# Layer two's norm and modulation inside its linear attention; layer one's output, norm and gate logits as one stage by tiles

## What is computed

```python
x = L0_attn_X
h = _layernorm(x, axis=-1) * (1 + ca) + sa
x = x + ga * _L0_attn_ref(h, ...)          # differential softmax attention, 16 heads of two maps
h = _layernorm(x, axis=-1) * (1 + cb) + sb # (A) layer one's second norm
x = x + gb * _L0_ffn_ref(h, ...)           # its experts: softmax(h @ wg), top 1024 tokens of each expert
...                                        # layer two: sa, ca, ga, sb, cb, gb from L1_c
h = _layernorm(x, axis=-1) * (1 + ca) + sa
x = x + ga * _L1_attn_ref(h, ...)          # linear attention
h = _layernorm(x, axis=-1) * (1 + cb) + sb # (B) layer two's second norm
x = x + gb * _L1_ffn_ref(h, ...)           # top-1 experts: softmax(h @ wg)

# end of _L0_attn_ref
O = jnp.einsum('bhqk,bhkd->bhqd', softmax(A1) - lam * softmax(A2), V)
rms = jnp.sqrt(jnp.mean(O * O, -1, keepdims=True) + EPS)
O = O / rms * rms_scale * (1.0 - LAMBDA_INIT)
return O.transpose(0, 2, 1, 3).reshape(B, N, H * 2 * dh) @ W_o.T
```

## Time and profile before

| what | us |
|---|---|
| median of 3 runs (3873.89 to 3878.0) | 3877.72 |
| the profiled execution | 3881.68 |
| its span, first to last instruction | 3879.9 |
| attention0, first DMA to the end of its last PE work | 229 to 2327 |
| out0, first DMA to the first of gates0 | 195.79 |
| gates0, first DMA to the first DVE instruction of route0 | 69.44 |
| linear1, first DMA to the first of gates1 | 230.4 |
| gates1, first DMA to the first instruction of route1 | 64.38 |

### The profile page before, as it was taken

One profiled execution on the slowest core, in us unless ns is written; L12 is line 12 of the kernel. 1 busy time (PEld: TensorE's weight loads), 2 busy tenths in 40 slices (PEclk: granted clock), 3 DMA queues, 4 the chain that ended last, 5 costly groups with the idle time before them and its releaser, 6 DMA issues. The chain is left out here.

```text
span 3879.9 us, 84027 instructions
## 1 busy us (share of the span) xinstructions
PE 3364.8 (87%) x27565; PEld 1836.3 (47%) x27567; DVE 2309.8 (60%) x5396; ACT 1639.4 (42%) x3358; POOL 1690.8 (44%) x1101
## 2 busy tenths in 40 slices
PE   7958999999999999999999995753799958985993
PEld 3413444444444444444444435642455536764662
DVE  4567777777777777777777715767311155665103
ACT  2514656565656565656666661110122235321110
POOL 1413656565656565656566673300344440211103
PEclk9968999999999999999999997855799979995996
DMA  5531111111111111111111104110433320002323
GB/s 180 196 108 25 48 39 42 40 39 43 37 43 36 45 34 46 33 48 31 50 32 47 31 10 144 47 45 0 126 82 78 59 58 5 1 6 95 100 92 97
DMA packets 229266, 224.78 MB, mean 58 GB/s; under 512 B 88722, under 2 KB 198547, under 8 KB 222739
## 3 DMA queue, kind: packets, MB, share of 16 engines
q1 hardware_dynamic: 213522, 194.34, 17.0%
q0 software_dynamic: 15360, 25.44, 3.4%
HBM read 138.58 MB, written 80.35 MB: 56 GB/s over the span
## 5 line engine op out<-in xcount | busy, mean ns | idle before, releaser
L669 POOL TENSOR_TENSOR attention_probs<-attention_probs 128x1024 f32<-128x1024 f32 (+2 forms) x640 | 1228.7, 1920 | 878.8 <-PE attention_ps_o L806 878.8
L699 ACT ACTIVATE attention_probs<-attention_ps_s 128x512 f32<-128x512 f32 (+3 forms) x2560 | 1197.3, 538 | 849.5 <-PE attention_ps_s L781 460.6
L729 DVE TENSOR_REDUCE attention_chunk_max<-attention_ps_m 128x1 f32<-128x512 f32 x1536 | 1006.0, 686 | 245.5 <-PE attention_ps_m L827 242.9
L827 PE MATMUL attention_ps_m<-attention_k_stack,attention_q_stack 96*128 96x512 bf16 (+3 forms) x2560 | 880.5, 359 | 46.0 <-DMA attention_v_head<-v_rows 36.8
L777 PE MATMUL attention_ps_s<-attention_q_stack,attention_k_stack 99*128 99x512 bf16 (+3 forms) x2560 | 801.2, 352 | 47.1 <-issue 34.1
L806 PE MATMUL attention_ps_o<-attention_probs,attention_v_head 128*32 128x256 f32 (+1 forms) x9728 | 637.9, 366 | 0.4 <-ACT attention_probs L699 0.4
L725 DVE CUSTOM_DVE_ANT_0 attention_ps_m<-attention_ps_m,attention_mask_wide 128x128 f32<-128x128 f32 (+3 forms) x1024 | 500.4, 498 | 229.2 <-PE attention_ps_m L827 210.5
L827 PEld LDWEIGHTS attention_ps_m<-attention_k_stack,attention_q_stack 96*128 96x128 bf16 x2560 | 244.2, 98 | 462.4 <-DVE attention_chunk_max L729 183.6
L817 PE MATMUL attention_ps_o<-attention_probs,consts 128*32 128x256 f32 (+1 forms) x5120 | 415.0, 360 | 0.4 <-POOL attention_probs L669 0.4
L777 PEld LDWEIGHTS attention_ps_s<-attention_q_stack,attention_k_stack 99*128 99x128 bf16 x2560 | 248.3, 98 | 313.0 <-ACT attention_probs L699 143.6
L806 PEld LDWEIGHTS attention_ps_o<-attention_probs,attention_v_head 128*32 128x32 f32 x9728 | 264.1, 110 | 270.5 <-issue 105.0
(11 more groups left out here) (279 smaller groups left out, 3593.1 us busy)
## 6 DMA issues: line engine op xcount, KB each, us to landing
qk_parts<-project_parts SPq DMA_DIRECT2D x64, 384.0 KB, 3.0
heads_out<-attention_results_sb SPq DMA_DIRECT2D x256, 64.0 KB
out_heads<-heads_out SPq DMA_DIRECT2D x8, 2048.0 KB, 7.9
experts_w<-in_f_w SPq DMA_DIRECT2D x16, 1024.0 KB, 8.4
attention_q_stack<-qk_parts SPq DMA_DIRECT2D x32, 384.0 KB
attention_k_stack<-qk_parts SPq DMA_DIRECT2D x32, 384.0 KB
experts_w<-in_e_w SPq DMA_DIRECT2D x24, 512.0 KB, 4.7
v_rows<-project_v SPq DMA_DIRECT2D x8, 1024.0 KB, 4.0
```

The lines of the kernel that those rows point to most:

```text
L669: pool.tensor_tensor(probs[:, to, :, lo:], probs[:, to, :, lo:], probs[:, k % RING_P, :, lo:], ALU.add).then_inc(pair_ok, 1)
L699: act.activation(probs[:, k % RING_P, a, left(k):], ps_s[(2 * k + a) % RING_S][:, left(k):], ACT.Exp, scale=float(DH) ** -0.5).then_inc(pr ...
L729: last = dve.tensor_reduce(to, ps_m[m % RING_M][:, 0:w], AX.X, ALU.max)
L827: pe.matmul(ps_m[m % RING_M][:, 0:w], qs[at][0:STACK, a, jq * P:(jq + 1) * P], ks[at][0:STACK, a, c * GROUP:c * GROUP + w], start=True, st ...
```

## The change

1. **Layer one.** out0 and gates0 become one stage, `out0_gates0`, written out for 32 tiles with no hardware loop. In round i every engine does one piece of work of several tiles at a time (tile i, i-1, ... as the lags say). The gate is multiplied into the output weights beforehand (one copy of the weights for each batch), so that DVE adds the projection to x in one instruction. POOL squares no longer: ACT does (Square), and POOL scales by the inverse root mean square in DVE's place. The norm, modulation, transposes and logits of a tile follow its projection. Both epsilons go into ACT's Sqrt as a bias.
2. **attention0** does what the stage needs first: SP loads lambdas, weights and scale behind the stacks of the first two heads (`load_weights`), and the first group's heads and sums at the start of the last head (`load_first_group`); lambda and the weights are made at the ends of ACT's and DVE's lists.
3. **Layer two.** linear1 norms and modulates a tile two chunks behind its mask, on DVE and ACT, and writes the result into the tile's place in `v`, whose values have been used by then; SP stores it. The loops get one more chunk of lag (`older`).
4. **gates1** becomes `logits1`: PE turns tiles of `v` at once, ACT and DVE copy a half each, PE forms logits; no norm, no stores.

```diff
@@ attention0 @@
+                if head is None:
+                    load_weights()
+                elif isinstance(head.n, int) and head.n == HEADS - 1:
+                    load_first_group()
...
+            act.wait_ge(lam_prod, 1)
+            act.activation(first.lam_two[:], first.lam_two[:], ACT.Exp).then_inc(lam_exp, 1)
...
+            chain.then(dve.tensor_scalar(first.w_in[:], first.w_in[:], first.scale[:, 0:1], 1.0 - LAMBDA_INIT,
+                                         ALU.mult, ALU.mult))
+            for b in range(B):
+                dve.tensor_tensor(first.w[:, b], first.w_in[:], core.rows[:, 0, b, GATE_A].unsqueeze(1)
+                                  .broadcast_to([P, DQ // P, D]), ALU.mult)
@@ out0_gates0: SP @@
+            def load(g):
+                at = g % RING_H
+                if g >= RING_H:
+                    sp.wait_ge(turned_h, (g - RING_H + 1) * GT)
+                    sp.wait_ge(turned_l, g - RING_H + 1)
...
+            load(1)
+            sp.dma_start(wg_sb[:], wg.rearrange("(k p) n -> p k n", p=P)).then_inc(wg_in, 16)
+            for i in range(T + 4):
+                if i % GT == 0 and i // GT + 2 < GROUPS:
+                    load(i // GT + 2)
+                if i >= 4:
+                    store(i - 4)
@@ ACT @@
+            for i in range(T + 5):
+                for lag, work in ((1, root), (2, copy_o), (3, deviation), (4, copy_x), (0, squares)):
+                    if 0 <= i - lag < T:
+                        work(i - lag)
@@ POOL @@
+            for i in range(T + 1):
+                if i < T:
+                    subtract(i)
+                if i >= 1:
+                    norm(i - 1)
@@ DVE @@
+            def add(t):
+                dve.wait_ge(y_ok, t + 1)
+                dve.tensor_tensor(core.x[:, t], ps_y, core.x[:, t], ALU.add).then_inc(x_ok, 1)
+
+            def statistics(t):
+                dve.wait_ge(x_ok, t + 1)
+                dve.bn_stats(stats[t % 2][:], core.x[:, t]).then_inc(stats_ok, 1)
+                dve.wait_ge(stats_ok, t + 1)
+                dve.bn_aggr(mv[t % RING_T][:], stats[t % 2][:]).then_inc(var_ok, 1)
...
+            for i in range(T + 4):
+                for lag, work in ((0, divide), (1, sum_squares), (3, add), (3, statistics), (3, centre),
+                                  (3, modulate), (1, invert_rms)):
+                    if 0 <= i - lag < T:
+                        work(i - lag)
+                    if lag == 0 and i % GT == GT - 1 and i // GT + 1 < GROUPS:
+                        invert(i // GT + 1)
@@ PE @@
+            def project(t):
+                pe.wait_ge(oT_ok, t + 1)
+                if t >= 1:
+                    pe.wait_ge(x_ok, t)
...
+            for i in range(T + 5):
+                for lag, work in ((0, turn), (3, project), (2, turn_back), (4, turn_x), (5, logits)):
+                    if 0 <= i - lag < T:
+                        work(i - lag)
+                if i % GT == 2 and i // GT + 1 < GROUPS:
+                    turn_totals(i // GT + 1)
@@ logits1: PE @@
+            turn(0)
+            pe.wait_ge(w_in, 16)
+            for g in range(B * NG):
+                if g + 1 < B * NG:
+                    turn(g + 1)
+                pe.wait_ge(hT_ok, g + 1)
+                pe.wait_ge(copied, g + 1)
...
@@ linear1 @@
+            def step(b, older, old, now, new, newer, at):
+                if older is not None:
+                    tile = older if isinstance(older, int) else sp.snap(older)
+                    wait_apart(sp, h_ok, older * 2 + 2, core.passed)
+                    sp.dma_start(h_view[:, ds(tile, 1)], v[:, ds(tile, 1)]).then_inc(h_out, 16)
+
+            run(sp, lambda b: None, step)
+            sp.wait_ge(h_out, T * 16)
@@ ACT, last in a step @@
+                if older is not None:
+                    act.wait_ge(var_ok, older + 1)
+                    act.activation(rstd[:], mv[:, 1:2], ACT.Sqrt, bias=eps[:, 0:1]).then_inc(std_ok, 1)
@@ DVE, behind the mask of `new` @@
+                if older is not None:
+                    wait_apart(dve, x_ok, older + 2, core.passed)
+                    row = core.x[:, ds(older, 1), :].rearrange("p a d -> p (a d)")
+                    dve.bn_stats(stats[:], row).then_inc(stats_ok, 1)
+                    wait_apart(dve, stats_ok, older + 1, core.passed)
+                    dve.bn_aggr(mv[:], stats[:]).then_inc(var_ok, 1)
+                    dve.wait_ge(var_ok, older + 1)
+                    dve.scalar_tensor_tensor(scaled[:], row, mv[:, 0:1], core.rows[:, 1, b, SCALE_B],
+                                             ALU.subtract, ALU.mult).then_inc(h_ok, 1)
+                    wait_apart(dve, h_ok, older * 2 + 1, core.passed)
@@ DVE, last in a step @@
+                if older is not None:
+                    dve.wait_ge(std_ok, older + 1)
+                    dve.reciprocal(rstd[:], rstd[:]).then_inc(rstd_ok, 1)
+                    dve.wait_ge(rstd_ok, older + 1)
+                    dve.scalar_tensor_tensor(v[:, ds(older, 1), :].rearrange("p a d -> p (a d)"), scaled[:], rstd[:, 0:1],
+                                             core.rows[:, 1, b, SHIFT_B], ALU.mult, ALU.add).then_inc(h_ok, 1)
```

More of the change, by code:

```diff
@@ L960, in _ @@
+            with nc.allow_non_contiguous_dma(reason="eight scores of a row"):
+                sp.dma_start(h_view[:, :, D:], scores[:]).then_inc(scores_out, 16)
+            for at in range(RING_T):
+                sp.wait_ge(stored[at], T // RING_T * 16)
+            sp.wait_ge(scores_out, 16)
         @block.scalar
         def _(act):
-            act.wait_ge(lam_prod, 1)
-            act.activation(lam_two[:], lam_two[:], ACT.Exp).then_inc(lam_exp, 1)
-            def step(now, after, at, pair):
-                if now is None:
-                    return
-                act.wait_ge(mean_ok, now + 1)
-                act.activation(mean[at][:], mean[at][:], ACT.Sqrt).then_inc(root_ok, 1)
-                for j in range(GT):
-                    act.wait_ge(y_ok, now * GT + j + 1)
-                    act.wait_ge(turned_o, now * GT + j + 1)
-                    act.activation(oT_sb[:, j % 2], ps_t[:], ACT.Copy).then_inc(oT_ok, 1)
@@ L1051, in step @@
-            def step(now, after, at, pair):
-                if now is not None:
-                    norm(now, at)
-                if after is not None:
-                    invert_totals(after)
-                    normalise(after, 0)
-                for j in range(GT):
-                    if after is not None and j + 1 < GT:
-                        normalise(after, j + 1)
-                    if now is not None:
-                        add(now, j, pair)
-                    if after is not None:
-                        squares_of(after, j, 1 - at)
@@ L1124, in _, with turn_x @@
[L1124 to L1137 removed]
+            def turn_x(t):
+                pe.wait_ge(h_ok, t + 1)
+                if t >= 1:
+                    pe.wait_ge(hT_ok, t)
+                for k in range(DC):
+                    last = pe.transpose(ps_x[:, k], h[t % RING_T][:, k * P:(k + 1) * P], core.c("ident"))
+                last.then_inc(turned_x, 1)
@@ L1138, in gates, with logits1 @@
+def logits1(nc, core, wg, h, scores):
+    with stage(nc, "gates1") as s:
+        w = s.sb("wg_sb", [P, DC, NE], F32)
+        hT = [s.sb(f"hT{i}", [P, DC, GROUP], F32) for i in range(2)]
         most = s.sb("most", [P, T], F32)
@@ L1913, in _, with step @@
         def _(act):
[L1914 removed]
+            act.wait_ge(ready, 1)
+            def step(b, older, old, now, new, newer, at):
                 if newer is not None:
```

502 lines of the change are left out of this document (253 added, 249 removed).

## The result

The changed kernel takes **3788.18 us** (median of 4 runs, 3785.34 to 3791.4) against 3877.86 for the kernel before beside it (3873.89 to 3880.64): a ratio of 0.977 with a 95% interval of 0.9753 to 0.9787. The forecast was 3808 in a range of 3772 to 3850: the sign, the range and most of the mechanism held, and 20 us more were gained than forecast. The time lies at the very edge of the 3788 to 3830 that the forecast gave to its own case. The profiled execution took 3789.88 us with a span of 3788.1, 91.8 shorter than before.

The account below looks back on a forecast made before the run. No engine was full in out0, gates0 or gates1; linear1 was nearly PE-bound. From the profiled execution, 3881.7 - 79 + 1 + 24 - 15 = 3812.7 us, less 4.0 for the runs' median, gave 3808, range 3772 to 3850.

Parts of the forecast that it names:

- its own case: Whole kernel: the forecast of 3808 us with its own range 3788 to 3830, Rival (d) included; chance 0.56.
- Part 1: Merged stage, out0's first DMA to route0: 265.2 us become 186.0 with DVE at 5.0 us a tile; gain 79 us.
- Part 2: attention0: early loads queue nothing, DVE's seven new operations may meet POOL's additions; 0 to 4 us, taken at 1.
- Part 3: linear1: the norm mostly fills DVE's waits, plus table loads, batch gap and end; costs 24 us (15 to 38).
- Part 4: logits1: PE without a break at the low clock, 49 us against gates1's 64.38; gain 15 us.
- PE's slack: Merged stage: PE's loop fits within DVE's round, 6.2 us against 6.95, leaving 0.8 us.
- DVE and POOL at SBUF: Merged stage: centring and shifting read two SBUF tensors beside POOL's work; priced at 0, at most 0.7 us a tile.
- the first batch's six passes load it again: linear1: ACT reloads the root's table once in each of six passes, 1.28 less about 0.45 each; 5 us.
- Rival (a): Merged stage: PE's clock keeps falling as in out0, mean 0.8, about 6.0 us a tile, +28, 3836; chance 0.19.
- Rival (b): Merged stage: transposes and eight-column matmuls hold PE at the low clock, 106 us more, 3914; chance 0.09.
- Rival (c): logits1: runs at the high clock as it has no waits, 44.3 becomes about 22 us, 3786; chance 0.16.
- Rival (d): linear1: the norm does not fit at all, costing 38 us or more, 3822 or more; inside the forecast's 0.56.

## Why the prediction was right, and what it mis-sized

| term | predicted, us | by the traces, us |
|---|---|---|
| Part 1, the merged stage | -79 | -95.8 |
| until the add of tile 0 | 20.4 | 18.8 |
| 28 tiles | 140 | 125.8 |
| the last three | 11 | 10.7 |
| behind the last add | 14.6 | 14.1 |
| Part 2, attention0 | +1 | -2.5, within the scatter |
| Part 3, linear1 | +24 | +29.2 |
| 26 chunks and the loads | 12 + 5 | 15.3 (first batch) + 4.0 (second) |
| between the batches | 2.5 | 4.5 |
| the end | 4.7 | 5.2 |
| Part 4, logits1 | -15 | -23.3 |
| sum | -69 | -92.4 |

- **Part 1** was right in its mechanism (no late start, DVE full, clock at 1.00) and its fixed terms are within 1.6 us. The mis-sized term is the pace: 5.0 us a tile, where 4.49 were measured, below the lower bound of 4.65. That bound laid records end to end. Start to start the same steps take 4.03 us, with a quarter of the inversions 4.39. The 0 to 0.6 us added for own waits were counted on top of this; such gaps are 0.03 to 0.1 us, inside the 4.03. In the other direction the wait of the division for the heads turned behind PE's sums, 0.6 us a group, had not been seen; the run with the sums moved shows it. PE's slack, put at 0.8 us a round, is 0.4 in a plain round and none around an inversion, as the run without statistics shows.
- The price of 0 for **DVE and POOL at SBUF** was nearly right: centring and shifting took 0.48 as before, between POOL's two operations. Only the second inversion took 0.54 us while POOL subtracted, against 0.23 in the first group, where POOL stood idle: 0.1 us a tile.
- **Part 2** can't be seen. The merged stage's first DMA stood between 2327.86 and 2334.72 in the kernels with the new attention0, and out0's at 2328.00 and 2333.79 in two with the old one: the same spread, some 7 us, from one execution to the next.
- **Part 3**: the waits for state, mask and y did vanish, and a chunk without loads costs 6.76 us, in the range of 6.70 to 7.00 but below the 6.88 taken; the second batch is 4.0 us longer (98.60 against 94.62 from its first to its last mask), not 6, the first 15.3 (109.41 against 94.12). The step that failed is "the first batch's six passes load it again": each pass has two loads, and the pair costs about 2 us a pass, 11.6 in all, not 5. The runs with and without the root's table first show it. The gap between the batches was 2 us under-sized. With the root's table first it is 1.2 us shorter, with PE's clock at 1.00 in its first 10 us and not 0.85; the other 0.8 stay open.
- **Part 4**: a group at the low clock takes 5.02 us, not 3.58 + 1.95, because the logits take 3.42 us there, and transposes and logits overlap by 0.2 us at each change; the stage at 0.50 throughout takes 44.4 us, not 49. That is the larger part of the 8 us; the other 3.3 are the first two groups at a higher clock.
- **Rival (a)** did not come, and the run with three memsets shows that the clock holds with still less work on PE. The prediction put out0's low clock down to the idle time during DVE's norm; its first fall came ahead of that. **Rival (b)** did not come either: with 14 transposes to eight projection records in each tile the stage ran at 1.00. The Trainium skill, "TensorE: Matmul & The Clock Gate", Part 4, says that transposes don't count as busy in the same way. That stage doesn't decide it, for it had projections too. Its opening speaks against it: from 2331.38 to 2338.12 PE did sums and transposes alone, and the clock was 0.58 in the last 3 us of them and 0.99 in the 3 us behind them. logits1, which had transposes and logits alone and fell to 0.50 without idle time, agrees with it. **Rival (c)** came in part, by 3.3 us, which changes from one execution to the next; with two idle products it comes for most of the stage. That the time stands next to its 3786 is chance: logits1 ran at 0.54, and the gain came from Part 1's pace. **Rival (d)** is the direction of Part 3's error.

The two errors of the forecast had opposite signs: 25 us too little gain in Parts 1 and 4, 5 us too little loss in Part 3. So the total came nearer than Parts 1 and 4 alone would have.

## What to carry to other kernels

Cost an engine that will be full by the distances between starts in a stretch where it is already full, not by the sum of its records' durations, and count a stall of the new order only where the next row shows an idle time. Ahead of a hardware loop whose body uses a function of another ACT table, run that function once: linear1's loop, entered with another table, had two loads in every pass, and none after one idle root. Where a stage of PE has short pieces only, look at its granted clock before its instruction count.

## What the runs showed of the hardware that was not expected

- logits1 with the same instructions took between 37.9 and 45.2 us in seven traces: its mean clock was 0.54 in the changed kernel and 0.50 in the one with the sums moved, though PE had no idle time between the groups in either. In four of the seven it rose early and fell again, in three it never rose. What decides it stays open; with two or four idle products a group it rose early and held 1.00 in three traces of three, with one it rose after some 16 us.
- logits1 got 8 us shorter with 32 records more on PE, 4.8 below the shortest of those seven.
- An inversion's follow-up on DVE with both inputs in SBUF, 128x64, took 0.23 us in the first group with POOL idle, and 0.53 to 0.54 in the other seven, each time beside POOL's subtraction.
